# Expert routing moved from its own block into the last batch of the attention, four tiles at a time, with a table by expert and rank

## The chip, the cores and the metric

The kernel runs on one core of a Trainium2 chip. The metric is device time in microseconds (us) of that core, from runs of the whole program. TensorE is called PE here, VectorE DVE, ScalarE ACT, GpSimd POOL and SyncE, which issues most DMAs, SP.

## The reference

One decoder layer over 8 x 256 tokens of width 512: a linear attention, a masked cross attention with 16 heads (both with a residual and a layer norm), and a mixture of 16 experts with the best four per token. What the change touches is the third part:

```python
logits = x @ router_weight.T + router_bias
top_val, top_idx = jax.lax.top_k(logits, TOP_K)
top_val = jax.nn.softmax(top_val, axis=-1)
router_scores = jnp.zeros_like(logits).at[jnp.arange(T)[:, None], top_idx].set(top_val)
gate_up = jnp.einsum('th,ehd->etd', x, gate_up_proj) + gate_up_proj_bias[:, None, :]
...
out = jnp.einsum('etd,edh->eth', (up + 1.0) * glu, down_proj) + down_proj_bias[:, None, :]
out = out * router_scores.T[:, :, None]
out = out.sum(axis=0)
```

## The kernel before, in words

The program is a row of blocks. At the end of a block every engine waits for all the others.

**`attention`** holds the first two parts. The cross attention goes through 8 batches (b) of 16 steps (s), four steps to a group of four heads. In a step PE makes two pairs of score matmuls (`scores`, L1219) into a ring of three PSUM banks (`RING`, `ring_bank`), ACT takes the exponential of each (`exps`, L705), PE multiplies those of two steps earlier with v (`values`, L1236), and PE makes the maxima's scores eight steps ahead (`scores_max`, L1204), which DVE reduces at once (`reduces`, L896), one pair of banks `ps_a` for each half. PE takes no further scores of the maxima until DVE has reduced the last ones. After the last batch's heads are made (`keep_o`), `spread_heads` (L1250) lays them out for two tiles of 128 tokens, DVE inverts the sums (L937), adds (L944 to L949) and normalizes. The tokens of tile t are `x[:, t]`, called x_keep in the profile. The order of all this is written out by hand in the loops over n of each engine; in the last batch `turn_x2` (L1260) turns tiles 10, 11, 12 and 13 at steps 4, 5, 14 and 15, and tiles 14 and 15 at the very end; `logits` (L1270) makes the router's logits of two tiles. POOL finishes the heads of the batch before (`finish_heads`, six instructions, L523 to L531), and raises variances to the power -1/2 (L536, L654, L658).

**`route`** begins when the logits of all 16 tiles stand. SP loads the first expert's weights (12 pieces, L1765), the biases, and stores all of x as the start of the sum (L1590) and zeros for the dummy rows (L1593, L1594), then loads the second expert's weights. ACT and POOL cut the first expert's weights in a high and a low part (`split_hi` L1776, `split_lo` L1785). DVE finds the best four of each token, PE ranks each choice among the earlier ones of its expert (L1724, L1726), DVE turns the ranks into places, an expert's places beginning at a multiple of 128 behind those of the expert before it. For each of 16 tiles DVE then makes two tables of ones and zeros (L1687, L1690) and a product (L1693), ACT another (L1617), and eight matmuls (L1734) add the tokens and their weights up to a list of 79 tiles of 128 places.

**`experts`** goes through those tiles, four to a round. ACT writes the numbers of the rows (`aim_from`, L1940), POOL gathers the rows three tiles ahead (`gather`, L1876), PE turns them (L2051) and makes three products of 12 matmuls (L2070): gate, up and, for the tile before, down. With the first tile of an expert, ACT and POOL also cut the next expert's weights. The weight of each row comes from the tables `weight` and `weight_a`. POOL scatters the results (L1886). **`last_norm`** is the last layer norm.

## Time and profile before

| what | us |
|---|---|
| median of three runs | 1603.31 (1599.92 to 1605.49) |
| the profiled execution | 1600.59 |
| its span | 1598.8 |
| busy PE / DVE / POOL / ACT | 1456.5 / 971.5 / 839.9 / 723.2 |
| matmuls of the experts, three groups of 912 | 231.8, 230.2, 231.6 |
| score maxima reduced by DVE, 256 | 300.3 |

The span is the profiled execution from its first to its last instruction. Times in the trace count from its start. A busy share is a mean over stages with different limits, so the stages are read one by one: the last batch up to 753, the end of the attention up to 769.7, the routing block up to 827.7, and the experts.

### The profile page before, as it was taken

Reading aid. Unit: us, or ns where it says so; the run is one execution under the profiler, and the core shown is the slowest. Engines: PE = TensorE matmul, PEld = TensorE weight load, DVE = VectorE, ACT = ScalarE, POOL = GpSimd, SP = SyncE. Lnnn points to the kernel's source line nnn. Section 1 sums busy time; section 2 is a strip of 40 time slices with the busy share of each in tenths; the row PEclk is TensorE's granted clock in tenths of the full one; section 3 lists DMA queues with packets and bytes.
Section 4 is the critical chain, followed back from the end, with each engine's and each line's share of the span. In section 5 each row is a group of like instructions: output and inputs, shape, how many; then the busy total and the mean of one; then the engine's idle time right before and its main releaser. Section 6 shows DMA issues by size and latency. Waiting matters only on the chain. (4 is left out here: it accounts for less than half of the span.)

```text
span 1598.8 us, 28732 instructions
## 1 busy us (share of the span) xinstructions
PE 1456.5 (91%) x7582; PEld 1031.8 (65%) x7583; DVE 971.5 (61%) x1389; ACT 723.2 (45%) x1348; POOL 839.9 (53%) x681
## 2 busy tenths in 40 slices
PE   6999999799999999998269999999999999999990
PEld 5878887444444444442257887777777877877770
DVE  2324344778887888886765555555555555555554
ACT  4212222278777778775223434424434443444223
POOL 4425333555666765632415536666666666486322
PEclk9999999799999999999579999999999999999996
DMA  6201022564557547530724445655556565473326
GB/s 212 72 14 49 13 49 54 80 89 72 99 113 123 109 84 132 89 64 30 275 75 121 118 92 151 160 151 155 151 151 158 148 161 151 110 191 80 59 54 223
DMA packets 92658, 179.04 MB, mean 112 GB/s; under 512 B 17032, under 2 KB 19848, under 8 KB 91944
## 3 DMA queue, kind: packets, MB, share of 16 engines
q1 hardware_dynamic: 72888, 132.76, 32.8%
q0 software_dynamic: 18544, 44.84, 14.2%
q8 instruction: 38, 0.62, 0.2%
q10 hardware_dynamic: 1152, 0.52, 0.2%
q14 instruction: 36, 0.29, 0.1%
HBM read 115.03 MB, written 33.46 MB: 93 GB/s over the span
## 5 line engine op out<-in xcount | busy, mean ns | idle before, releaser
L896 DVE TENSOR_REDUCE stage<-ps_a 128x2 f32<-128x1024 f32 x256 | 300.3, 1218 | 80.2 <-PE ps_a L1204 79.6
L705 ACT ACTIVATE probs<-ps_b 128x512 f32<-128x512 f32 x512 | 278.0, 595 | 54.4 <-PE ps_b L1219 52.0
L1785 POOL TENSOR_TENSOR we_split<-we_raw,we_split 128x512 f32 (+1 forms) x192 | 250.5, 1543 | 97.3 <-ACT we_split L1776 95.2
L2070 PE MATMUL ps_y<-we_split,hT 128*128 x912 | 231.8, 403 | 4.3 <-DVE hT L2001 3.4
L2070 PE MATMUL ps_g<-we_split,xT 128*128 x912 | 230.2, 401 | 5.0 <-issue 4.3
L2070 PE MATMUL ps_u<-we_split,xT 128*128 x912 | 231.6, 403 | 0.0
L2070 PEld LDWEIGHTS ps_g<-we_split,xT 128*128 128x128 f32 x912 | 171.8, 190 | 52.9 <-issue 12.9
L2070 PEld LDWEIGHTS ps_y<-we_split,hT 128*128 128x128 f32 x912 | 166.2, 189 | 41.8 <-issue 7.2
L2070 PEld LDWEIGHTS ps_u<-we_split,xT 128*128 128x128 f32 x912 | 166.3, 189 | 34.8
L1936 ACT ACTIVATE hT<-ps_h 128x512 fp32r<-128x512 f32 x76 | 45.3, 597 | 296.5 <-PE ps_h L2051 240.3
L1886 POOL DMA_INDIRECT scratch_acc<-x_keep,to_rows x76 | 121.2, 1595 | 109.7 <-issue 51.6
L1219 PE MATMUL ps_b<-stack 55*128 55x512 f32 x512 | 131.0, 505 | 15.9 <-ACT probs L705 11.1
L1236 PE MATMUL ps_pv<-probs,v_aug 128*32 128x512 f32 x1024 | 139.7, 619 | 0.0
L1876 POOL DMA_INDIRECT x_rows<-scratch_x,from_rows x79 | 78.7, 997 | 112.7 <-ACT from_rows L1940 86.1
L1219 PEld LDWEIGHTS ps_b<-stack 55*128 55x128 f32 x512 | 50.8, 188 | 132.1 <-ACT probs L705 114.4
L2022 DVE TENSOR_TENSOR ps_g<-ps_g,we_bias 128x512 f32<-128x512 f32 x76 | 53.2, 700 | 115.7 <-PE ps_g L2070 80.4
L2013 DVE SCALAR_TENSOR_TENSOR x_keep<-ps_y,slot_weight_a,bw 128x512 f32<-128x512 f32 x76 | 57.1, 751 | 95.2 <-PE ps_y L2070 91.9
L2028 DVE TENSOR_TENSOR ps_u<-ps_u,we_bias 128x512 f32<-128x512 f32 x76 | 53.2, 700 | 88.4 <-PE ps_u L2070 88.4
L1930 ACT ACTIVATE xT<-ps_x 128x512 fp32r<-128x512 f32 x78 | 46.8, 600 | 119.0 <-PE ps_x L2051 119.0
L1204 PE MATMUL ps_a<-stack 53*128 53x512 f32 x512 | 90.9, 422 | 10.3 <-DVE stage L896 10.3
L1318 PE MATMUL ps_b<-stack,xT_split 128*128 128x512 f32 x384 | 93.2, 394 | 0.0
L1776 ACT ACTIVATE we_split<-we_raw 128x2048 f32 (+1 forms) x48 | 88.4, 1904 | 3.1 <-DMA we_raw<-in_w_expert 3.1
(254 smaller groups left out, 2213.8 us busy)
## 6 DMA issues: line engine op xcount, KB each, us to landing
we_raw<-in_w_expert SPq DMA_DIRECT2D x192, 256.0 KB
stack<-xT_raw SPq DMA_DIRECT2D x192, 128.0 KB, 5.4
we_bias<-in_b_expert SPq DMA_DIRECT2D x16, 768.0 KB, 4.0
stage<-in_w SPq DMA_DIRECT2D x5, 1024.0 KB, 4.9
xT_raw<-in_xT SPq DMA_DIRECT2D x4, 1024.0 KB, 6.4
x_tok<-in_x POOLq DMA_DIRECT2D x16, 256.0 KB, 3.1
scratch_acc<-x_keep SPq DMA_DIRECT2D x1, 4096.0 KB, 18.0
acc_sb<-scratch_acc SPq DMA_DIRECT2D x8, 512.0 KB, 6.6
```

The lines of the kernel that those rows point to most:

```text
L705: nc.scalar.activation(probs[:, n % 3, h], src[:], ACT.Exp, scale=DH ** -0.5).then_inc(b_kept, 1)
L896: nc.vector.tensor_reduce(out[:, :, i, k % NC], ps_a[i][:], AX.X, ALU.max, negate=True).then_inc(a_kept[i], 1)
L1204: mm = nc.tensor.matmul(ps_a[i][:, e], q_stack[rows, slot, p, c * P:(c + 1) * P], k_stack[rows, slot, p, :], start=True, stop=True)
L1219: nc.tensor.matmul(out[:], k_stack[rows, slot, p, c * P:(c + 1) * P], q_stack[rows, slot, p, :], start=True, stop=True).then_inc(b_made, 1)
L1236: mm = nc.tensor.matmul(ps_pv[32 * h:32 * h + 32, :], v_aug[:, b % 2, c, 4 * g + h, :], probs[:, n % 3, h], start=(c == 0), stop=(c == NC ...
L1318: mm = nc.tensor.matmul(out[:], xT_split[:, xi, c, i * P:(i + 1) * P], w_split[w][:, wi, c, :], start=(n == 0), stop=(n == 3 * KC - 1))
L1776: nc.scalar.activation(dst, W["raw"][:, k], ACT.Copy).then_inc(W["hi"], 1)
L1785: nc.gpsimd.tensor_tensor(lo, W["raw"][:, k, c], hi, ALU.subtract).then_inc(W["lo"], 1)
L1876: pool.indirect_dma_start(x_rows[j][:], None, S["x2"], bass.IndirectOffsetOnAxis(from_rows[j][:], 0))\
L1886: pool.indirect_dma_start(S["acc"], bass.IndirectOffsetOnAxis(to_rows[j][:], 0), y[j], None, compute_op=ALU.add).then_inc(added, 16)
L2013: nc.vector.scalar_tensor_tensor(y[j], ps_y[:], pick(W["weight_a"], i), bw[:, j % 2], ALU.mult, ALU.add).then_inc(y_ready, 1)
L2070: mm = nc.tensor.matmul(out[:], left[:, a, c], w[:, bass.ds(par, 1), k, b, c].squeeze(1), start=(n == 0), stop=(n == len(passes) - 1))
```

## The change

The routing is cut into four groups of four tiles. Groups 0 to 2 are routed inside the last batch of the attention, group 3 in the block `route`.

- DVE: `top_experts`, `chosen_experts` and `rank_slots` of a group take the place of the long instructions over all 16 tiles. Each instruction whose result the next one needs is followed by a wait (`chain`). PE ranks a group with two matmuls (`rank_tokens`); ACT copies the ranks out of the ring and takes the exponentials (`keep_rank`, `raise_shares`).
- A choice's place is now expert x 16 + rank / 128 in a table of 256 columns, so the matmuls that add up the table (`spread_tile`, four to a tile, fp32r) need no totals. Their operands are products of digit tables (`mark_tile`, two instructions to a tile): on POOL for tiles 0 to 11, on DVE for the last four. The table lies in the bank that held the attention's values.
- `route` loses the 16-tile loop. A few small instructions and matmuls turn the counts into `tile_place`, `tile_expert` and the rest. Of the first expert's weights POOL cuts there only the gate's, and only after all marks; up and down are cut at the start of `experts`, behind the first three gathers. The second expert's load moves to the start of `experts`.
- The rows' weights are stored beside x in DRAM (`store_weights`, 32 more columns, so a gathered row has 544 elements). ACT picks a tile's weights from the gathered rows (`keep_weight`) with one register load, and `aim_from` and `aim_to` have a register load each for the place.
- From step 8 of the last batch the ring of scores has five banks: the three, and the two of `ps_a[0]`, free once the last maxima are reduced. `spread_heads` uses `ps_a[1]` alone for both tiles. `make_head_rows` moves ahead of the last reduction.

```diff
+        WIDER = USE["exp", N - LEAD, 0]
+        late_ring = [ps_b[(WIDER + i - EARLY) % RING][:] for i in range(RING)] + [ps_a[0][:, 0], ps_a[0][:, 1]]
...
+                if b == B - 1:
+                    pool.wait_ge(b_made, USE["exp", STEPS * b - 1, 3] + 1)
+                    for t in range(8):
+                        mark_tile(nc.gpsimd, pool, R, K, t, in_tiles[t], of_tiles[t])
                 if b >= 1:
                     finish_heads(b - 1)
...
+            for t in range(8, 10):
+                mark_tile(nc.gpsimd, pool, R, K, t, in_tiles[t], of_tiles[t])
             pool.wait_ge(y2_moments, B - 1)
             nc.gpsimd.tensor_tensor(rstd2[:], mean_var2[:, :, 1], minus_half2[:], ALU.pow).then_inc(y2_rstd, 1)
             for o in range(2):
+                if o == 1:
+                    for t in range(10, EARLY_TILES):
+                        mark_tile(nc.gpsimd, pool, R, K, t, in_tiles[t], of_tiles[t])
...
                 b, s = n // STEPS, n % STEPS
+                if b == B - 1 and s == 7:
+                    make_head_rows()
                 if n + LEAD < N:
                     reduces(n + LEAD)
...
+                    top_experts(nc, dve, R, K, s // 2, s // 2)
+                if b == B - 1 and s in (1, 3):
+                    chosen_experts(nc, dve, R, K, s // 2, s // 2)
+                if b == B - 1 and s in (5, 6):
+                    dve.wait_ge(b_kept, USE["rank", s - 5] + 1)
+                    rank_slots(nc, dve, R, K, s - 5, s - 5, K["rank"][:, (s - 5) % 2])
+            dve.wait_ge(b_kept, USE["logits", 5] + 1)
+            top_experts(nc, dve, R, K, 2, 2)
+            chosen_experts(nc, dve, R, K, 2, 2)
             invert_spread(0)
             invert_spread(1)
             moments(B - 2)
...
             add_spread(0)
+            dve.wait_ge(b_kept, USE["rank", 2] + 1)
+            rank_slots(nc, dve, R, K, 2, 2, K["rank"][:, 0])
             dve.wait_ge(y2_rstd, B - 1)
...
+def mark_tile(compute, engine, R, K, t, in_tile, of_tile, at=None):
...
+    if t % 4 == 0:
+        engine.wait_ge(R["slots_made"], t // 4 + 1)
+    compute.tensor_tensor(in_tile.rearrange("p k (m l) -> p k m l", l=16),
+                          K["mid_tok"][:, at, ks].unsqueeze(3).to_broadcast([P, K_TOP, 8, 16]),
+                          K["low"][:, at, ks].unsqueeze(2).to_broadcast([P, K_TOP, 8, 16]),
+                          ALU.mult).then_inc(R["marked"], 1)
+    compute.tensor_tensor(of_tile, K["chosen"][:, at, ks].unsqueeze(3).to_broadcast([P, K_TOP, E_, n]),
+                          K["hi"][:, at, ks, 0:n].unsqueeze(2).to_broadcast([P, K_TOP, E_, n]),
+                          ALU.mult).then_inc(R["marked"], 1)
...
+            pool.wait_ge(R["marked"], 2 * NT)
+            split_lo(nc, pool, W, 0, 0, 0, range(KC))
```

DVE, the second half of the last batch's steps with maxima. Before, the engine goes from the reductions to the head rows and the inversions (stage<-ps_a are the reduced maxima, kv_mask the head rows, full the inverted sums):

```order
L896 TENSOR_REDUCE stage<-ps_a 128x2 x6
L905 CAST stage<-stage 128x2x8
L907 TENSOR_TENSOR stage<-stage 128x2x8
L930 COPY kv_mask<-ident 128x128
L937 RECIPROCAL full<-ps_a 64x512 x2
L918 BN_STATS stats<-late 128x6 x2
```

Now, from step 6 on:

```order
L934 TENSOR_REDUCE stage<-ps_a 128x2 x2
L1718 TENSOR_TENSOR stage<-stage,w_qk 128x256
L1719 TENSOR_REDUCE stage<-stage 128x16
...
L1734 TENSOR_TENSOR stage<-stage,token 128x128
L968 COPY kv_mask<-ident 128x128
L934 TENSOR_REDUCE stage<-ps_a 128x2 x2
L943 CAST stage<-stage 128x2x8
L945 TENSOR_TENSOR stage<-stage 128x2x8
L1676 TENSOR_TENSOR logits<-logits,rb 128x64
...
L1702 COPY carry<-stage 128x16
L975 RECIPROCAL full<-ps_a 64x512 x2
```

The inversions stand behind all of group 1's slots (L1718 to L1734, eleven instructions) and group 2's choices (L1676 to L1702, 15 instructions).

POOL, the last batch. Before:

```order
L523 TENSOR_TENSOR late<-late,u_sb 128x512 x2
L527 TENSOR_TENSOR late<-late 128x512 x2
L531 TENSOR_TENSOR late<-late,x_keep 128x512 x2
L654 TENSOR_TENSOR rstd<-mean_var,minus_half 128x2
L658 TENSOR_TENSOR rstd<-mean_var,minus_half 128x1 x2
```

Now (L1747 and L1751 are `mark_tile`'s two instructions; of the 16 for tiles 0 to 7 the last two are shown):

```order
L1747 TENSOR_TENSOR in_tile_low<-stage 128x512
L1751 TENSOR_TENSOR stack<-stage,w_qk 128x512
L543 TENSOR_TENSOR late<-late,u_sb 128x512 x2
L547 TENSOR_TENSOR late<-late 128x512 x2
L551 TENSOR_TENSOR late<-late,x_keep 128x512 x2
L1747 TENSOR_TENSOR in_tile_low<-stage 128x512
L1751 TENSOR_TENSOR stack<-stage,w_qk 128x640
L1747 TENSOR_TENSOR in_tile_low<-stage 128x512
L1751 TENSOR_TENSOR stack<-stage,w_qk 128x640
L680 TENSOR_TENSOR rstd<-mean_var,minus_half 128x2
```

The heads of batch 6 stand behind the marks of tiles 0 to 7, and the power for tiles 12 and 13 behind the marks of tiles 8 and 9.

## Rows read from the trace of the kernel before

**Rows 1.** Windows by stage: length, busy time of each engine, TensorE's granted clock, DMA share, GB/s.

```profile
697.00:728.00 31.00, 25.72 (x157) 10.65 (x157) 24.32 (x27) 20.19 (x40) 14.16 (x11) 0.90 0.15 41
769.00:828.00 59.00, 24.85 (x134) 21.25 (x134) 53.79 (x144) 15.23 (x23) 16.90 (x15) 0.70 0.59 215
845.00:1545.00 700.00, 693.67 (x3252) 557.52 (x3251) 403.13 (x593) 270.48 (x490) 416.68 (x327) 1.00 0.53 134
```

**Rows 2.** Timeline of DVE, end of the last batch: start, us, instruction, idle before.

```profile
724.59 1.19 DVE L907 TENSOR_TENSOR stage<-stage 128x16 fp32r<-128x16 f32 x1
725.71 1.35 DVE L930 COPY kv_mask<-ident 128x128 f32<-128x128 f32 x1
729.13 3.35 DVE L937 RECIPROCAL full<-ps_a 64x512 f32<-64x512 f32 x1 [2.08 <-PE ps_a L1250]
737.34 3.36 DVE L937 RECIPROCAL full<-ps_a 64x512 f32<-64x512 f32 x1 [4.86 <-PE ps_a L1250]
742.33 0.17 DVE L923 TENSOR_SCALAR mean_var<-mean_var 128x2 f32<-128x2 f32 x1
744.50 1.00 DVE L962 TENSOR_SCALAR x_keep<-late,mean_var,rstd 128x512 f32<-128x512 f32 x2
```

**Rows 3.** Timeline of POOL: heads of batch 6, power for tiles 12 and 13, first expert's weights.

```profile
725.71 2.48 POOL L531 TENSOR_TENSOR late<-late,x_keep 128x512 f32<-128x512 f32 x2
742.58 1.13 POOL L654 TENSOR_TENSOR rstd<-mean_var,minus_half 128x2 f32<-128x2 f32 x1 [14.39 <-DVE mean_var L923]
777.74 16.45 POOL L1785 TENSOR_TENSOR we_split<-we_raw,we_split 128x512 fp32r<-128x512 f32 x12 [7.60 <-ACT we_split L1776]
```

**Rows 4.** Groups by line and shape, 690 to 820: busy us, mean ns, idle before.

```profile
L1645 DVE TENSOR_REDUCE sel<-chosen 128x256 f32<-128x1024 f32 x1 | 1.9, 1871 | 0.0
L1635 DVE MAX8 top<-logits 128x8 f32<-128x16 f32 x16 | 1.3, 158 | 0.1
L1131 DVE TENSOR_TENSOR logits<-logits,rb 128x256 f32<-128x256 f32 x1 | 0.4, 424 | 4.2 <-ACT logits L724 4.2
L1639 DVE TENSOR_TENSOR gap<-top 128x64 f32<-128x64 f32 x1 | 0.2, 209 | 0.0
```

**Rows 5.** Timeline of DVE in the routing block, beside POOL's twelve instructions of rows 3.

```profile
783.31 0.22 DVE L1656 TENSOR_REDUCE total<-share 128x16 f32<-128x64 f32 x1
788.40 1.17 DVE L1669 TENSOR_TENSOR base<-tile_end,n_tiles 128x16 f32<-128x16 f32 x1
790.82 0.42 DVE L1671 TENSOR_TENSOR place<-ps_r,base 128x256 f32<-128x256 f32 x1
```

**Rows 6.** Timeline of ACT: pairs of exponentials in a step without maxima.

```profile
738.68 1.09 ACT L705 ACTIVATE probs<-ps_b 128x512 f32<-128x512 f32 x2 [1.28 <-PE ps_b L1219]
741.35 1.09 ACT L705 ACTIVATE probs<-ps_b 128x512 f32<-128x512 f32 x2 [0.22 <-PE ps_b L1219]
```

**Rows 7.** Routing block: SP's last store and POOL's first instruction; landing times from the DMA view.

```profile
769.78 0.20 POOL L1602 MEMSET ones<- 128x128 f32 x1 [5.70 <-POOLq L104]
787.41 2.70 SPq L1594 DMA_DIRECT2D scratch_acc<-zero  x1
scratch_acc<-zero SPq DMA_DIRECT2D x1, 256.0 KB, 9.8
```

**Rows 8.** Start of the experts: first instruction, last of three gathers, first product.

```profile
827.73 0.10 POOL L1899 MEMSET zero_row<- 128x1 f32 x1 [33.55 <-POOLq L1527]
831.20 0.95 POOL L1876 DMA_INDIRECT x_rows<-scratch_x,from_rows  x1 [0.30 <-issue]
836.92 5.07 PE L2070 MATMUL ps_g<-we_split,xT 128*128 x12 [1.24 <-issue]
```

**Rows 9.** A tile in which the next expert's weights are cut.

```profile
1039.87 0.19 ACT L1940 ACTIVATE from_rows<-slot_token 128x1 uint32 x1
1039.96 0.58 ACT L1936 ACTIVATE hT<-ps_h 128x512 fp32r<-128x512 f32 x1
1040.57 0.69 DVE L2001 TENSOR_TENSOR hT<-ps_h,hT 128x512 fp32r<-128x512 f32 x1 [0.16 <-ACT hT L1936]
1042.27 3.04 PE L2070 MATMUL ps_y<-we_split,hT 128*128 x12
```

More of the change, by code:

```diff
@@ new lines, in choice_buffers, with sb, chain @@
+def choice_buffers(nc, ctx):
+    def sb(name, shape, dt=F32):
+        return ctx.enter_context(nc.sbuf_tensor(f"late_{name}", shape, dt))[:]
+    views = {name: sb(name, (P, 1) + shape) for name, shape in CHOICE_SHAPES}
+    for name, shape in CHOICE_TEMPS:
+        views[name] = sb(name, (P,) + shape, U32 if name == "top_i" else I32 if name in ("slot_i", "digit_i") else F32)
+    views["hi"] = sb("hi", (P, 1, 4 * K_TOP, E_))
+    views["ones"] = sb("ones", (P, P))
+    return views
+def chain(R, dve, instruction):
+    R["done"][0] += 1
+    instruction.then_inc(R["step"], 1)
+    dve.wait_ge(R["step"], R["done"][0])
@@ new lines, in spread_tile, with raise_shares @@
+def spread_tile(nc, pe, R, table, t, in_tile, of_tile):
+    pe.wait_ge(R["marked"], 2 * t + 2)
+    columns = table[:, 0:PLACES].rearrange("p (e h) -> p e h", e=E_)[:, :, 0:of_tile.shape[-1]]
+    for k in range(K_TOP):
+        mm = nc.tensor.matmul(columns, in_tile[:, k], of_tile[:, k], start=(t == 0 and k == 0),
+                              stop=(t == NT - 1 and k == K_TOP - 1), skip_group_check=True)
+    mm.then_inc(R["spread_done"], 1)
+def raise_shares(nc, act, R, gap, g):
+    act.wait_ge(R["sel_made"], g + 1)
+    nc.scalar.activation(gap, gap, ACT.Exp).then_inc(R["raised"], 1)
@@ new lines, in store_weights, with tile_tables, sb @@
+def store_weights(sp, S, R, weights, g, groups):
+    sp.wait_ge(R["weights_made"], 1 if g == 0 else 2)
+    rows = S["x2"][4 * g * P:4 * (g + groups) * P, D:D + 2 * E_]
+    sp.dma_start(rows.rearrange("(t p) e -> p t e", p=P), weights.rearrange("p g t x -> p (g t) x")).then_inc(
+        R["weights_stored"], 16)
+def tile_tables(nc, ctx):
+    def sb(name, shape, dt):
+        return ctx.enter_context(nc.sbuf_tensor(name, shape, dt))
+    return {
+        "token": sb("place_token", [P, PLACES + 1], U32),
+        "place": sb("tile_place", [1, TILES], I32),
+        "expert": sb("tile_expert", [1, TILES], I32),
+        "active": sb("tile_active", [1, TILES], I32),
+        "new": sb("tile_new", [1, TILES], I32),
+        "parity": sb("tile_parity", [1, TILES], I32),
+        "last_tile": sb("expert_last", [1, E_], I32),
+    }
@@ L1963, in _ @@
                 aim_from(j, j)
-            x_hi(0, 0)
-            x_hi(1, 1)
+            for j in range(2):
+                x_hi(j, j)
+                keep_weight(j, j)
             def body(i, j):
@@ L1981, in body @@
                 weigh_bias(i, j, par)
+                if not (isinstance(i, int) and i >= TILES - 2):
+                    keep_weight(i + 2, (j + 2) % U)
                 if not is_at(i, 0):
```

491 lines of the change are left out of this document (282 added, 209 removed).

## The prediction

> **What bounds the kernel now.** I read the windows by stage first. In the experts PE is busy 693.67 of 700 us [rows 1]: there only PE's work counts, and the change leaves it alone. In the routing block PE has 24.85 of 59 us and DVE 53.79: DVE's row of instructions is that block, 58.0 us from POOL's first instruction at 769.78 to the first of the experts at 827.73 [rows 7, 8]. The last batch comes next. There PE has 25.72 of 31 us, DVE 24.32 and POOL 14.16 [rows 1]. PE cannot make the maxima's scores of a step before DVE has reduced those of the last one, so DVE has only 31 - 24.3 = 6.7 us to give before it holds PE. Then I read the timelines of DVE and POOL there, because that is where the work goes, and asked which chain leads to the end: head rows, two inversions, moments, power on POOL, and x_keep of tiles 12 and 13 at 744.50 [rows 2], which PE needs in step 14 and without which nothing behind it (turn, logits, spread, tiles 14 and 15) starts.
>
> **The end of the attention, up to the first inversion.** DVE gets, before its inversions, three times `top_experts`, three times `chosen_experts` and twice `rank_slots`. From the groups [rows 4]: an instruction of 64 columns takes 0.21, of 256 columns 0.42, the sixteen MAX8 1.3 together, the strided reduction of 1024 columns 1.87, and I give each `chain` wait 0.04.
> - `top_experts`: 0.21 + four MAX8 0.4 + four index searches 0.6 (an estimate, half as much again as the MAX8) + 0.21 + 0.2 + gaps = 1.7, three times 5.1.
> - `chosen_experts`: 0.42 + a quarter of 1.87 = 0.5 + a scan of 80 columns and two small copies 0.5 + gaps = 1.6, three times 4.8.
> - `rank_slots`: three of 256 columns 1.3, a reduction 0.4, two of 128 columns 0.6, five small ones 0.7, gaps 0.3 = 3.3, twice 6.6.
> - constants 0.9. Sum 17.4 us if nothing else runs.
>
> Something else runs. While POOL does its twelve instructions of 1.2 to 1.4 us (16.45 in all), an instruction of 16 columns takes DVE 1.17 us, where a reduction takes 0.22 and one with a PSUM operand 0.42 [rows 3, 5]. The same shows at 724.59 and 725.71, beside POOL's heads: 1.19 and 1.35 [rows 2, 3]. So a small DVE instruction that reads SBUF twice, or copies, waits for the end of POOL's current one, about 1.0 us each. The change puts 16 marks and the six heads, some 24 us of POOL work without a break, beside DVE from the moment group 0's slots are made: beside group 1's slots (7 instructions of the waiting kind until POOL runs out of marks for group 0), two of the maxima, and the 8 such of group 2's choices. That is 17 with those; three of them more or less, and three waits are there today (two of some 1.1 in these rows, and the cast ahead of them: 2.9 together), so 17 x 1.0 - 2.9 = 14.1.
>
> The Trainium skill says the same as a rule against this change (SBUF — State Buffer, Who interferes with whom): VectorE with two SBUF inputs, or in a 2-port mode, and GpSimd reading SBUF lock each other out for a whole instruction. The rows above bear it out, reductions and PSUM operands included. Read alone, it would let me price a wait at half an instruction, 0.6 us; then the 17 cost 10 in place of 17 and the whole comes out near 1600. The rows show nearly the full length each time, since DVE's next instruction arrives just after POOL's next has begun, so I keep 1.0.
>
> The first inversion, now at 729.13, so moves by 17.4 + 14.1 - 6.7 (DVE's idle time) - 2.1 (its wait for the spread heads, [rows 2]) + 1 for handovers that stay = 23.7 us.
>
> **Up to tiles 12 and 13.** The second inversion waits 4.86 us for step 10 today [rows 2]; by then it will not: -4.9. The heads of batch 6 end at 728.2 today [rows 3]; behind the marks they end some 30 later, at about 758, still ahead of the moments. From the variance (742.50) to x_keep (744.50) it is 2.0 us now, since the power (1.13) runs beside `add_spread`. Then it will be `add_spread` 2.1 with its handovers, `rank_slots` of group 2 3.3, POOL's marks of tiles 8 and 9, 2 x (1.25 + 1.55 for 640 columns) = 5.6, the power 1.1, handovers 0.3: 12.4, so +10.4. Sum: 23.7 - 4.9 + 10.4 = 29.2.
>
> **The ring of five.** Two pairs of exponentials take 2 x 1.09 = 2.2 us, and a step 741.35 - 738.68 = 2.7 [rows 6]: the ring could give 0.5 x 8 = 4 us. I count nothing, as PE will stand in step 14 for x_keep anyway, some 20 us. The head rows' move ends a stall of PE at step 8, with the same answer. `spread_heads` on one pair waits for `add_spread(0)`, done before x_keep: nothing.
>
> **Behind x_keep.** 24 us lead from 744.50 to the last logits today. They stay, and PE starts them after a long wait; in the routing block, where it waits as much, it was granted 0.70 of its clock [rows 1]. Add twelve table matmuls (tiles 9 to 11) before the last logits: +0.7, `share_weights` partly hidden, colder matmuls +1. Sum +1.7. The attention ends 29.2 + 1.7 = 31 us later.
>
> **The routing block.** DVE's row is then: choices of group 3 with constants 3.8, weights 1.7, slots 3.3, marks 4 x (0.7 + 1.2) = 7.6 (512 and 1024 columns, estimates by 0.42 for 256), counts and tables about 9, of which 4 are waits beside POOL's four cuts: 26 us with the start. But SP's zeros, issued at 787.41, land 9.8 later, at 797.2, which is 27.5 us after the block's start [rows 7], behind the same 3 MB of weights and 4 MB of x that stay. So the DMAs become the block's end: 27.5 + 0.8 for the last weights and the barrier = 28.3, in place of 58.0: -29.7. Bounds: 27.5 if the small store lands in time, 34 if DVE's small instructions wait more often.
>
> **The experts.** The first product starts 9.2 us after the block does [rows 8]. It now needs POOL's low part of the up weights, cut behind the third gather: 831.20 + 0.95 + 4 x 1.25 + 0.3, that is 9.7 to 10: +1 with what follows on ACT in the first tile. `keep_weight` and two register loads stand ahead of the cut of the next expert's weights. In such a tile ACT's hT starts at 1039.96, DVE's part ends at 1041.26, and PE comes to it at 1042.27 [rows 9]: 0.9 us of slack with the handover in each of 14 changes of expert. No row shows a load alone; from below nothing, as three loads between two ACT instructions at 1039.87 and 1039.96 cost nothing seen; from above some 2 us a tile, 14 x 1.2 = 17. I take +1, nearest to the row. The 6% longer gathered row costs nothing at a DMA share of 0.53.
>
> **Sum.** 31 - 29.7 + 1 + 1 = +3.3 us, so 1603.9 for the profiled execution of 1600.59. The median of the runs is 2.7 above that execution, so I forecast 1606.6, rounded to **1607**: the routing block loses half its time and the last batch gets it all back. About 0.3% (4.8 us) can be told from no change, so the line lies at 1598.5 and 1608.1.
>
> **Rivals.**
> - *The work hides (faster).* If DVE's small instructions seldom meet POOL's, the 14.1 goes; DVE then waits for batch 6's heads behind the marks, which gives back about 4. The attention ends 21 later, time 1597; if the slots' own 10 us hid too, 1588. For it: DVE has 6.7 us idle, and 7 more in its waits for spread heads. Against: two rows of 1.19 and 1.35 in this very place.
> - *The marks cost more than 1.25 us (slower).* They have four-dimensional broadcast operands, and no row shows one on POOL. Tiles 0 to 7 hold DVE and the heads, tiles 8 and 9 lie in the chain itself. At 1.3 times the price the chain grows by 6.5 us (3 in waits on DVE and the heads, 1.7 in tiles 8 and 9, the rest in tiles 10 and 11 ahead of the last power), time 1613; at 1.6 times by 15, 1622. Slower than can be missed from 1.1 times on.
> - *Register loads in the experts (slower).* 14 x up to 1.2 us: up to 1624. For it nothing but the order of instructions.
>
> **Chances.** Forecast, 1599 to 1615: 0.50, of which 0.28 within 0.3% and 0.22 above. Hidden: 0.30, all faster. Marks: 0.15. Loads: 0.05. Faster 0.30, same 0.28, slower 0.42. The range 1590 to 1622 leaves out the deepest part of the first rival and the ends of the other two; the forecast's own is 1599 to 1615.
>
> **What would show it.** The routing block 28 us long, its end released by a DMA. DVE's first inversion 20 us or more later against step 0 of the last batch, small instructions of 1.0 to 1.3 us beside POOL's marks. PE idle for more than 10 us before the turn of tile 12, released by x_keep. Pairs of exponentials closer together than 1.35 us in steps 9 to 13. Wrong would be: x_keep of tile 12 less than 20 us later, marks far from 1.25 us for 512 columns, or an experts' stage longer by over 3 us.

## The result, and the profile of the changed kernel

| | kernel before | changed kernel |
|---|---|---|
| median of 20 runs each, us | 1600.7 | 1605.5 |
| all runs, us | 1592.9 to 1607.0 | 1603.5 to 1609.4 |
| profiled span, us | 1598.8 | 1604.6 |
| ratio of the times | | 1.0035, 95% interval 1.0023 to 1.0047 |

The change makes the kernel slower by 0.35%, just more than the 0.3% that can be told from no change. The forecast was 1607, and 0.42 stood on slower. But the sum that gave it was right only as a whole: the last batch up to the first inversion was forecast 7.7 us too high and the experts 8.6 us too low. That the two cancel is luck.

This is where the time went, from one profile of each kernel. The marks in time are ACT's first exponentials of the last batch (693.89 and 692.45), DVE's first inversion, the variance and x_keep of tiles 12 and 13, POOL's first instruction of the routing block, POOL's first of the experts, the 76 instructions of DVE that finish a tile (`finish`), and the end.

| stretch | before | after | difference | forecast |
|---|---|---|---|---|
| up to step 0 of the last batch | 693.9 | 692.5 | -1.4 | 0 |
| from there to DVE's first inversion | 35.2 | 51.3 | +16.0 | +23.7 |
| from there to the variance | 13.2 | 8.4 | -4.8 | -4.9 |
| variance to x_keep of tiles 12, 13 | 2.2 | 10.8 | +8.6 | +10.4 |
| x_keep to the routing block | 25.3 | 28.9 | +3.6 | +1.7 |
| routing block | 58.0 | 28.5 | -29.5 | -29.7 |
| experts, to the first finished tile | 28.8 | 32.2 | +3.3 | +1 |
| first to 75th tile, 15 changes of expert | 700.0 | 707.3 | +7.3 | +1 |
| the last interval | 6.8 | 9.6 | +2.8 | 0 |
| behind the last tile | 35.5 | 35.4 | -0.1 | 0 |
| sum | | | +5.8 | +3.3 |

The two marks of step 0, the kernel before first:

```profile
693.89 1.09 ACT L705 ACTIVATE probs<-ps_b 128x512 f32<-128x512 f32 x2 [0.89 <-PE ps_b L1219]
```

```profile
692.45 1.09 ACT L734 ACTIVATE probs<-ps_b 128x512 f32<-128x512 f32 x2 [0.39 <-PE ps_b L1279]
```

Windows by stage of the changed kernel, with the columns of [rows 1]: the last batch up to the first inversion, the routing block, the experts.

```profile
697.00:744.00 47.00, 37.20 (x201) 13.98 (x193) 45.17 (x114) 26.08 (x55) 25.34 (x25) 0.89 0.10 28
791.00:820.00 29.00, 7.16 (x34) 5.37 (x34) 18.53 (x66) 6.18 (x5) 5.15 (x5) 0.50 0.91 331
845.00:1545.00 700.00, 688.44 (x3209) 550.00 (x3208) 397.14 (x584) 286.46 (x556) 414.37 (x326) 1.00 0.54 135
```

In the last batch DVE is now busy 45.17 of 47 us: it became the bound, and its idle time of [rows 1] is used up. In the experts the same 700 us hold 5.2 us less of PE's work than before. The share of busy time falls from 99.1% to 98.3%, too little to notice on the page, but as large as the whole loss.

The timeline of DVE in the last batch, against [rows 2]:

```profile
725.81 0.42 DVE L1719 TENSOR_REDUCE stage<-stage 128x16 f32<-128x256 f32 x1
726.26 0.83 DVE L1720 CAST stage<-stage 128x16 int32<-128x16 f32 x1
...
735.54 0.41 DVE L1678 MAX8 stage<-logits 128x8 f32<-128x16 f32 x4
...
738.56 1.47 DVE L1690 TENSOR_TENSOR stage<-iota_f,stage 128x256 f32<-128x256 f32 x1
...
743.70 6.74 DVE L975 RECIPROCAL full<-ps_a 64x512 f32<-64x512 f32 x2
...
752.08 0.17 DVE L961 TENSOR_SCALAR mean_var<-mean_var 128x2 f32<-128x2 f32 x1
...
762.83 1.00 DVE L1000 TENSOR_SCALAR x_keep<-late,mean_var,rstd 128x512 f32<-128x512 f32 x2 [5.42 <-POOL rstd L680]
```

and of POOL, against [rows 3]: the two marks of tile 7 (L1747 and L1751), the heads of batch 6, then marks of tiles 8 and 9 and the power.

```profile
736.41 1.05 POOL L1747 TENSOR_TENSOR in_tile_low<-stage 128x512 fp32r<-128x512 f32 x1
737.42 1.06 POOL L1751 TENSOR_TENSOR stack<-stage,w_qk 128x512 fp32r<-128x512 f32 x1
738.45 2.70 POOL L543 TENSOR_TENSOR late<-late,u_sb 128x512 f32<-128x512 f32 x2
...
758.51 1.29 POOL L1751 TENSOR_TENSOR stack<-stage,w_qk 128x640 fp32r<-128x640 f32 x1
...
762.01 0.72 POOL L680 TENSOR_TENSOR rstd<-mean_var,minus_half 128x2 f32<-128x2 f32 x1
```

The cast of 16 columns takes 0.83 us beside a mark, where the free one takes 0.17. The four MAX8 and the reduction keep their 0.41 and 0.42: they are not held. The two inversions stand back to back, so PE's spread heads are no longer waited for. And x_keep waits 5.42 us for POOL, which makes marks from 757.50 on and comes to the power at 762.01.

PE behind it (the views' line numbers are those of the changed kernel; L1761 is `spread_tile`):

```profile
763.43 1.11 PE L1321 MATMUL ps_b<-ident,x_keep 128*128 128x128 f32 x4 [12.45 <-DVE x_keep L1000]
...
779.78 6.24 PE L1761 MATMUL table<-stack,in_tile_low 128*128 128x64 f32 x28
785.82 1.05 PE L1321 MATMUL ps_a<-ident,x_keep 128*128 128x128 f32 x4
```

PE stands 12.45 us, then works almost without a break to the end of the stage. x_keep of tile 15 is there at 781.9, but its turn comes at 785.82, behind the products of tiles 2 to 8.

The routing block ends as forecast. These are the last issue of SP, DVE's last instruction and POOL's first of the experts, and from the DMA view the landing time of the last store:

```profile
812.41 2.67 SPq L1793 DMA_DIRECT2D scratch_x<-late_weights  x1
812.48 0.23 DVE L1916 SCALAR_TENSOR_TENSOR tile_new<-expert_f,new_f 1x79 int32<-1x79 f32 x1
820.15 0.10 POOL L2100 MEMSET zero_row<- 128x1 f32 x1 [8.02 <-POOLq L1817]
```

```profile
scratch_x<-late_weights SPq DMA_DIRECT2D x1, 64.0 KB, 7.3
```

DVE is through at 812.7; the last store, issued at 812.41, lands 7.3 us later, and the block ends at 820.15.

In the experts the difference sits at the changes of expert. ScalarE before and after in the same tile (the kernel before first), from the bias over the cuts of the next expert's weights to the next hT:

```profile
1204.47 0.71 ACT L1950 ACTIVATE bw<-we_bias,slot_weight 128x512 f32 x1
1205.09 0.19 ACT L1944 ACTIVATE to_rows<-slot_token 128x1 uint32 x1
1205.18 5.51 ACT L1776 ACTIVATE we_split<-we_raw 128x2048 f32 x3
1210.59 0.19 ACT L1940 ACTIVATE from_rows<-slot_token 128x1 uint32 x1
1210.68 0.58 ACT L1936 ACTIVATE hT<-ps_h 128x512 fp32r<-128x512 f32 x1
```

```profile
1205.18 0.71 ACT L2165 ACTIVATE bw<-we_bias,row_weight 128x512 f32 x1
1205.79 0.19 ACT L2158 ACTIVATE row_weight<-x_rows 128x2 f32 x1
1206.21 0.20 ACT L2152 ACTIVATE to_rows<-place_token 128x1 uint32 x1 [0.23 <-issue]
1206.59 5.53 ACT L1975 ACTIVATE we_split<-we_raw 128x2048 f32 x3 [0.17 <-issue]
1212.01 0.18 ACT L2147 ACTIVATE from_rows<-place_token 128x1 uint32 x1
1212.10 0.58 ACT L2139 ACTIVATE hT<-ps_h 128x512 fp32r<-128x512 f32 x1
```

The cuts start 0.71 us behind the bias before, 1.41 after. The loads in front of `from_rows` cost nothing here, hidden behind 5.5 us of cuts. hT is 0.7 later against the bias, and then PE:

```profile
1217.31 3.06 PE L2288 MATMUL ps_g<-we_split,xT 128*128 x12 [0.58 <-issue]
```

Before, the same gate product follows the down product at once; now it comes 0.58 us late. In an undisturbed tile the interval is 9.27 us in both kernels; in this one it is 10.13 against 9.41.

### The profile page after: what moved, and what is told of

Same layout as the page of the kernel before. It is cut to its first block and busy times, and to the rows that moved or that the text cites. A ratio compares the mean times of both kernels' runs of the same rounds, so it can differ in the third digit from the quotient of the medians.

```text
span 1604.6 us, 29621 instructions
## 1 busy us (share of the span) xinstructions
PE 1454.8 (91%) x7542; PEld 1028.6 (64%) x7543; DVE 966.7 (60%) x1414; ACT 738.4 (46%) x1416; POOL 862.1 (54%) x704
## 5 line engine op out<-in xcount | busy, mean ns | idle before, releaser
L734 ACT ACTIVATE probs<-ps_b 128x512 f32<-128x512 f32 x498 | 270.5, 595 | 50.3 <-PE ps_b L1279 44.1
L2288 PE MATMUL ps_y<-we_split,hT 128*128 x912 | 235.4, 407 | 6.0 <-DVE hT L2219 3.5
L1279 PE MATMUL ps_b<-stack 55*128 55x512 f32 x498 | 127.7, 502 | 16.7 <-ACT probs L734 8.2
L1296 PE MATMUL table<-probs,v_aug 128*32 128x512 f32 x1024 | 138.8, 615 | 0.5 <-ACT o_pair L742 0.5
L2231 DVE SCALAR_TENSOR_TENSOR x_keep<-ps_y,row_weight,bw 128x512 f32<-128x512 f32 x76 | 57.1, 751 | 94.1 <-PE ps_y L2288 94.1
L1264 PE MATMUL ps_a<-stack 53*128 53x512 f32 x512 | 90.2, 417 | 15.7 <-DVE stage L934 15.4
```

The lines of the kernel that those rows point to most:

```text
L734: nc.scalar.activation(probs[:, n % 3, h], src[:], ACT.Exp, scale=DH ** -0.5).then_inc(b_kept, 1)
L1264: mm = nc.tensor.matmul(ps_a[i][:, e], q_stack[rows, slot, p, c * P:(c + 1) * P], k_stack[rows, slot, p, :], start=True, stop=True)
L1279: nc.tensor.matmul(out[:], k_stack[rows, slot, p, c * P:(c + 1) * P], q_stack[rows, slot, p, :], start=True, stop=True).then_inc(b_made, 1)
L1296: mm = nc.tensor.matmul(ps_pv[32 * h:32 * h + 32, :], v_aug[:, b % 2, c, 4 * g + h, :], probs[:, n % 3, h], start=(c == 0), stop=(c == NC ...
L2231: nc.vector.scalar_tensor_tensor(y[j], ps_y[:], weight[:, j, 1:2], bw[:, j % 2], ALU.mult, ALU.add).then_inc(y_ready, 1)
L2288: mm = nc.tensor.matmul(out[:], left[:, a, c], w[:, bass.ds(par, 1), k, b, c].squeeze(1), start=(n == 0), stop=(n == len(passes) - 1))
```

## The experiments

Each line of a diff is against the changed kernel, if nothing else is said. First four that undo or move one part, in one series; the kernel before took 1599.9 there.

**1. The power ahead of the marks.**

```
-            for t in range(8, 10):
-                mark_tile(nc.gpsimd, pool, R, K, t, in_tiles[t], of_tiles[t])
             pool.wait_ge(y2_moments, B - 1)
...
-                    for t in range(10, EARLY_TILES):
+                    for t in range(8, EARLY_TILES):
...
             add_spread(0)
-            dve.wait_ge(b_kept, USE["rank", 2] + 1)
-            rank_slots(nc, dve, R, K, 2, 2, K["rank"][:, 0])
...
             last_norm(B - 1, 0, last_step)
+            dve.wait_ge(b_kept, USE["rank", 2] + 1)
+            rank_slots(nc, dve, R, K, 2, 2, K["rank"][:, 0])
```

> The changed kernel, with the power for tiles 12 and 13 issued on POOL ahead of the marks of tiles 8 and 9 (these go behind the power of tile 14), and the third rank_slots on DVE behind the normalization of tile 14. Nothing is left out. Theory: x_keep of tiles 12 and 13 is late because DVE ranks group 2 (754.2 to 757.4 in the changed kernel) and POOL makes two pairs of marks (757.5 to 762.0) before the power. With the swap x_keep follows the residual add at once: 754.3 plus about 0.8 for the power, so at about 755 instead of 762.8, and since PE stands 12.45 us there and works almost without a break behind it, the attention ends 7 to 8 us earlier: 1598 us. Rival A: the time behind x_keep is set by DVE (inversions of 3.4 us, the rank now between them, and waits beside POOL), which gives 3 to 4 us of it back: 1602. Rival B: x_keep 7 us earlier moves nothing, since PE's own work up to the end was what counted: 1605.

Measured: 1598.4 us, ratio to the kernel before 0.9994 (0.9983 to 1.0005), where the changed kernel has 1.0035: 6.6 us less (8.5 against the second series' 1.0047 of run 5). x_keep stands at 757.91 here; PE's turn in it:

```profile
758.50 0.88 PE L1319 MATMUL ps_b<-ident,x_keep 128*128 128x128 f32 x4 [3.30 <-DVE x_keep L998]
```

From the first inversion (747.36 here) to x_keep it takes 10.6 us in place of 19.1, so 8.6 less: the term of the table. From x_keep to the block it takes 28.5, as before the edit. The theory holds, and both rivals fall.

**2. ScalarE's order in the experts.**

```
...
                 nc.scalar.activation(glu[:], ps_g[:], ACT.Silu, scale=ALPHA).then_inc(glu_made, 1)
+                if not (isinstance(i, int) and i >= TILES - 1):
+                    keep_weight(i + 1, (j + 1) % U)
+                if not below(i, 2):
+                    aim_to(i - 2, (j - 2) % U)
                 if not (isinstance(i, int) and i >= TILES - 2):
                     x_hi(i + 2, j)
                 weigh_bias(i, j, par)
-                if not (isinstance(i, int) and i >= TILES - 2):
-                    keep_weight(i + 2, (j + 2) % U)
-                if not is_at(i, 0):
-                    aim_to(i - 1, (j - 1) % U)
...
```

> The changed kernel, with the experts' ScalarE order changed alone: the copy of a row's weights and the aiming of the scatter, with the register loads ahead of them, stand behind the SiLU, where ScalarE waits 1.5 us for PE, instead of between the bias and the cut of the next expert's weights. Nothing is left out. Theory: of the changed kernel's 5.8 us over the kernel before, 7.4 us arise at the 15 changes of expert, 0.5 us each: the cuts start 0.70 us later, the next hT is late by as much, PE's down product is released later and its sequencer has no lead left at the loop's branch (a gap of 0.58 us in front of the gate product). With the cuts where they were these gaps shrink to those of the kernel before: 6 to 7 us less, 1599 us. Rival A: the register loads cost wherever they stand (ScalarE or the loop's branch carries them): 1605. Rival B: the gaps come from the 544-wide gathers or the earlier weight loads, not from ScalarE: 1605 too, with hT on time.

Measured: 1600.0 us, ratio 1.0001 (0.9988 to 1.0014). The 74 intervals take 701.7 us, against 707.3 in the changed kernel and 700.0 before. ScalarE in a tile with a change, behind the cuts:

```profile
1207.82 0.59 ACT L2139 ACTIVATE hT<-ps_h 128x512 fp32r<-128x512 f32 x1
1208.39 0.60 ACT L2194 ACTIVATE glu<-ps_g 128x512 f32<-128x512 f32 x1
1209.10 0.21 ACT L2158 ACTIVATE row_weight<-x_rows 128x2 f32 x1
1209.80 0.20 ACT L2152 ACTIVATE to_rows<-place_token 128x1 uint32 x1 [0.49 <-issue]
```

The loads are still there, and cost 0.49 us and more of ScalarE's time, but in its wait for PE. 5.6 of the 7.3 us are gone. Both rivals fall: the loads and the copy cost by their place, and gathers and weights' loads are as in the changed kernel. The run does not part the loads from the copy `keep_weight`, which moves with them.

**3. A ring of three banks.**

```
-        late_ring = [ps_b[(WIDER + i - EARLY) % RING][:] for i in range(RING)] + [ps_a[0][:, 0], ps_a[0][:, 1]]
+        late_ring = [ps_b[(WIDER + i - EARLY) % RING][:] for i in range(RING)]
```

> The changed kernel with three banks in the ring of scores for the last steps too, as in the kernel before. Nothing is left out. Theory: the ring of five lets PE reach the turn of tile 12 earlier (751.0 in the changed kernel), where it stands 12.45 us for DVE, so the two banks are worth nothing: 1605.5, within 0.3% of the changed kernel, with a shorter stand before the same turn. Rival: the wider ring feeds DVE's last row maxima and the heads earlier, so that without it the heads' inversion is later by a step's difference: 1608 to 1612.

Measured: 1606.6 us, ratio 1.0036 (1.0024 to 1.0049): the same as the changed kernel. PE's stand in front of the turn of tile 12 shrinks from 12.45 us to 8.67:

```profile
768.21 1.12 PE L1321 MATMUL ps_b<-ident,x_keep 128*128 128x128 f32 x4 [8.67 <-DVE x_keep L1000]
```

What the steps lose is taken from the wait. From step 0 of the last batch to the first inversion it takes 53.7 us here. Five profiles with the ring of five and the same code up to there have 51.3 to 53.3, so the rival has nothing for it that this run could tell from the spread.

**4. The accumulator stored early.**

```
             store_x2(B - 3)
+            sp.dma_start(S["acc"][0:(NT - 4) * P, :].rearrange("(t p) d -> p t d", p=P),
+                         x[:, 0:NT - 4, :]).then_inc(x2_stored, 16)
...
-            sp.dma_start(S["acc"][0:TOK, :].rearrange("(t p) d -> p t d", p=P), x[:]).then_inc(acc_stored, 16)
+            sp.dma_start(S["acc"][(NT - 4) * P:TOK, :].rearrange("(t p) d -> p t d", p=P),
+                         x[:, NT - 4:NT, :]).then_inc(acc_stored, 16)
```

> The changed kernel, with the accumulator's rows of tiles 0 to 11 (3 MB of 4 MB) stored during the last steps of the attention, where the DMA engines are busy for 0 to 20% of the time, instead of in the routing block. Nothing is left out. Theory: the routing block of 28.5 us waits for its transfers (DVE is through at 812.7, the block ends at 820.15, the DMA engines are full from about 800 on); with 3 MB at 406 GB/s less, 7.4 us of transfers go, and the block ends where DVE and the last store of weights (landed about 815) set it: 5 us less, 1600.5 us. Rival A: the end is set by the descriptors of the zeros, 9.89 us of issue, not by the bytes: 1604 to 1605. Rival B: the early store delays the stores of x_keep and the last loads of the attention, and gives the gain back: 1605.

Measured: 1600.3 us, ratio 1.0001 (0.9988 to 1.0013), so 5.4 us less. The block runs from 792.48 to 814.00, 21.5 us in place of 28.5. SP and DVE in it:

```profile
800.68 0.62 SPq L1860 DMA_DIRECT2D scratch_x<-zero  x1
```

```profile
813.28 0.23 DVE L1919 SCALAR_TENSOR_TENSOR tile_new<-expert_f,new_f 1x79 int32<-1x79 f32 x1
```

DVE's last instruction ends 0.5 us ahead of the barrier: the bound passed from the transfers to DVE. Note the issue of the zeros: 9.89 us in the changed kernel, 0.62 here with the same descriptors. It shrank with the bytes ahead of it, so rival A took a wait for work. The block gains 7.0 us and the whole 5.4; 0.7 of the difference is that the first product comes 12.0 us after the experts' start in place of 11.3: PE takes up the first gathered rows 5.7 us after the gather is issued, in place of 5.0.

**5. The changed kernel again**, in a second series with runs 6 to 8; the kernel before took 1600.4 there.

> The changed kernel again, unchanged, beside the next three on one chip. Theory: what differs from run to run of one kernel is the early attention (up to 2.4 us between two profiles of edits that do not touch it) and whether PE's clock has fallen before the very last product (9.59 us against 6.8 us of the last interval between two results). So this run gives 1605.5 within 1.5 us, intervals of 9.59 or less at the end, and 707 to 708 us for the 74 intervals before it. Rival: those 707 us are themselves luck of a profile, and another one shows 700 to 703 as the kernel before.

Measured: 1608.7 us, ratio 1.0047 (1.0030 to 1.0064), 3.2 us above the 1605.5 that I gave and outside the 1.5 us that I allowed. The 74 intervals take 707.7 us, the last 8.5. The first inversion comes at 747.47, 3.8 us later than in the first profile. 3.5 of that lie ahead of the last batch: from its step 0 on it is 51.5 us here and 51.3 there. So times of single profiles are compared here from mark to mark only.

**6. The kernel before with the register loads.** The diff is against the kernel before; `own` holds each tile's own number.

```
             def aim_to(i, j):
-                nc.scalar.activation(to_rows[j][:], pick(G["token"], i), ACT.Copy).then_inc(to_set, 1)
+                at = act.value_load(pick(W["own"], i), min_val=0, max_val=TILES - 1)
+                nc.scalar.activation(to_rows[j][:], pick(G["token"], at), ACT.Copy).then_inc(to_set, 1)
...
+            def keep_like(i, j):
+                e = act.value_load(pick(G["expert"], i), min_val=0, max_val=E_ - 1)
+                nc.scalar.activation(kept[:, j], pick(G["weight"], e), ACT.Copy)
...
                 weigh_bias(i, j, par)
+                if not (isinstance(i, int) and i >= TILES - 2):
+                    keep_like(i + 2, (j + 2) % U)
```

(`aim_from` likewise.)

> The kernel before, with the register loads of the change alone: on ScalarE the aiming of gather and scatter goes through a table that holds each tile's own number (one more register load each, which the copy's address depends on), and a copy of 128x1 at an address from a loaded register stands between the bias and the aiming of the scatter. Nothing is left out and the results are the same. Theory: ScalarE in front of the cuts is what the experts' 7.4 us come from, so the kernel before takes on 6 to 7 us: 1606 to 1607 us, with the cuts 0.7 us behind the bias and gaps in front of the gate product of 0.58 us. Rival: the loads cost only together with the gathers of 544 columns or the earlier weights: below 1602.

Measured: 1610.0 us, ratio 1.0066 (1.0047 to 1.0085), so 9.6 us more than the kernel before, where I had expected 6 to 7. The 74 intervals take 707.6 us against 700.0, and look like those of the changed kernel. Another 1.8 stand ahead of the first finished tile: the first gather is issued 0.6 us later behind the register loads, and the first down product takes 4.59 us in place of 3.06. ScalarE at a change:

```profile
1207.33 0.71 ACT L1957 ACTIVATE bw<-we_bias,slot_weight 128x512 f32 x1
1207.95 0.19 ACT L1951 ACTIVATE row_kept<-slot_weight 128x1 f32 x1
1208.38 0.20 ACT L1947 ACTIVATE to_rows<-slot_token 128x1 uint32 x1 [0.24 <-issue]
1208.76 5.52 ACT L1778 ACTIVATE we_split<-we_raw 128x2048 f32 x3 [0.18 <-issue]
```

It is 1.43 us from bias to cuts, as good as the 1.41 of the changed kernel, without a wider gather and with the old order of the weights' loads. With run 2 this settles it: the cause is what stands on ScalarE ahead of the cuts, a copy and register loads together. Which of the two costs more was not tested.

**7. The table's bank free.** On top of run 1:

```
+                if s == 14 and b == B - 1:
+                    pe.wait_ge(o_kept, NG * B - 1)
+                    for t in range(0, 8):
+                        spread_tile(nc, pe, R, table, t, in_tiles[t], of_tiles[t])
                 if s in (4, 5, 14, 15) and b == B - 1:
                     turn_x2(2 * b - 4 + (4, 5, 14, 15).index(s))
```

and the last head group's sums in `ps_a[0][:, 1]`, which leaves the ring.

> The kernel of the run with the power first, with the last head group's values summed in one of the two banks that the ring of five had taken (the ring has four), so that the place table's bank is free, and the products that spread tiles 0 to 7 stand ahead of the turn of tile 12, where PE waits, instead of behind the turn of tile 14. Nothing is left out. Theory: behind x_keep of tile 12 PE works without a break up to the end, and 6.5 us of that are these products; PE has 3.3 us of waiting in front of the turn, so 3.3 us are gained and the rest is only moved: 1595 us. Rival A: the products delay the turn of tile 12, the spreading of heads 2 and DVE's last inversions by 3 us, and DVE's chain from there (invert, add, moments, power) is what ends the attention: no gain, 1598.4. Rival B: four banks in place of five let the steps before lag by over 2 us: 1600.

Measured: 1598.0 us, ratio 0.9984 (0.9972 to 0.9996), where run 1 has 0.9994: 1.6 us less, not 3.4, and the two intervals overlap, so the times alone do not show a gain. From x_keep of tile 12 to the block it takes 26.3 us in place of 28.5, so 2.2 less. The last turn now waits for DVE and no longer behind products:

```profile
775.89 1.12 PE L1323 MATMUL ps_b<-ident,x_keep 128*128 128x128 f32 x4 [0.40 <-DVE x_keep L999]
```

So the theory and rival A were each partly right: PE's own work was the bound, and after 2.2 us DVE's chain of the last tiles took over.

**8. All four edits together.**

> The changed kernel with all four edits together: the power first, ScalarE's order in the experts, the accumulator's rows of tiles 0 to 11 stored early, the table's bank free and the products of tiles 0 to 7 ahead of the turn of tile 12. Nothing is left out. Theory: they touch different stretches (attention's end, experts, routing block) and add up: 7 + 5.7 + 5.3 + 3 us off 1605.5, so 1584.5 us, faster than the kernel before by 1%. Rival: the routing block that starts earlier waits for the weights' load or DVE in any case, and the experts' first product is bound by the weights of the first expert, so that only 12 to 14 us come through: 1592.

Measured: 1582.0 us, ratio 0.9875 (0.9854 to 0.9896). The attention's gain, the block of 21.5 us and 700.3 us for the 74 intervals are all there. By stretches of the profiles the parts add up, each in its own: 8.6 + 2.2 + 7.0 + 7.0 = 24.8 us, where the ratios give 25.6. By whole times they do not quite: the single runs gave 8.2 (run 7 with run 1 in it), 5.4 and 5.4, so 19.0. The four executions of this run leave 22 to 29, and the rest is not explained. This version beats both kernels: by 18 us the kernel before, beside which it ran, and by 1.6% the changed one, by their ratios.

**9. No marks beside the ranking.** On top of run 1:

```
                     pool.wait_ge(b_made, USE["exp", STEPS * b - 1, 3] + 1)
-                    for t in range(8):
-                        mark_tile(nc.gpsimd, pool, R, K, t, in_tiles[t], of_tiles[t])
...
-                    for t in range(8, EARLY_TILES):
+                    for t in range(EARLY_TILES):
```

> The kernel of the run with the power first, with the marks of tiles 0 to 7 also moved, behind POOL's power of tile 14, so that POOL works on nothing but the heads while DVE ranks group 1 and chooses the experts of group 2. Nothing is left out. It is not meant to be faster: POOL then makes all 24 marks behind the power, about 24 us, and PE's products wait for them. Theory: DVE's small instructions of 0.8 to 1.5 us (rank_slots of group 1 took 5.6 us against 3.25 us for the same of group 0, the choice of group 2 9.3 us against 3.5 us) are waits beside POOL's marks and heads; without the marks the ranking takes 3.3 us again, and the first inversion comes 18 to 21 us behind the inversion of batch 6 instead of 27; the choice stays slow where it lies beside POOL's heads. The whole takes 1603 to 1612. Rival: the instructions are slow for another reason (the clock, the ring, their own data), keep their durations, and the first inversion stays at 27.

Measured: 1603.4 us (one run), the first inversion 23.5 us behind the inversion of batch 6 (718.48 to 741.97), not 26.9 as in the changed kernel or 27.5 as in run 1, but outside my 18 to 21. The details are the opposite of what I wrote. Without the marks POOL's heads, released earlier, lie beside the ranking of group 1, and the choice of group 2 is free:

```profile
726.65 2.89 POOL L543 TENSOR_TENSOR late<-late,u_sb 128x512 f32<-128x512 f32 x2 [15.61 <-PE ps_b L1275]
```

```profile
732.07 1.20 DVE L1720 CAST stage<-stage 128x48 f32<-128x48 int32 x1
733.30 1.29 DVE L1727 TENSOR_TENSOR stage<-iota_f,stage 128x128 f32<-128x128 f32 x1
734.63 0.43 DVE L1728 TENSOR_TENSOR w_qk<-iota_f,stage 128x256 f32<-128x256 f32 x1
...
739.80 0.21 DVE L1678 TENSOR_TENSOR stage<-logits,stage 128x64 f32<-128x64 f32 x1
```

The ranking takes 8.7 us in place of 5.6, the choice 3.4 in place of 9.3. So the rival falls: the same instructions are slow or quick with nothing changed but what POOL does at that time. Which of POOL's work it is doesn't matter, but its length does: beside heads of some 1.25 us a held instruction loses 0.5 to 1.1 us here; beside marks of 0.4 to 1.06 us it loses 0.2 to 0.9 in the changed kernel.

## Why the prediction came out, and where its steps did not

The number and the direction came out. The mechanism did so in part: the routing block, the chain to x_keep and the ring were read rightly, and two errors of some 8 us cancelled by luck. Of the prediction's own signs of being wrong, one came plainly: the experts' stage is longer by 10.6 us up to the 75th tile, where 3 was the line. One came narrowly: x_keep of tile 12 is 18.3 us later, or 19.8 from step 0 of the last batch, where less than 20 was to be wrong. The marks of 512 columns take 1.05 us in place of 1.25. The first inversion, which was to be 20 us or more later from step 0, is 16.0 later.

**The first inversion: +23.7 forecast, +16.0 measured** from step 0 of the last batch. The step that failed is "17 x 1.0 - 2.9 = 14.1". In the changed kernel 13 instructions are held by 0.2 us or more, and lose 9.0 us together over their free durations, 0.69 each; minus the 2.9 of before that is +6.1. With it the sum gives 15.7. This is from one pair of profiles: the second profile of the changed kernel has 51.5 us for the stretch, that of run 6, which has the attention of before, 34.1. I had read one row of 1.17 and two of [rows 2] and priced every wait at a whole instruction of POOL. The estimate of 0.6 us, half an instruction, that I had drawn from the Trainium skill (SBUF — State Buffer, Who interferes with whom) and set aside is near the 0.69; as to which instructions are held and which are spared, trace and rule agree. I counted the MAX8, the index searches and the reductions right, as free.

**The second inversion: -4.9.** As forecast, back to back.

**Variance to x_keep: +10.4 forecast, +8.6 measured.** The mechanism is right, and run 1 shows it by taking it away. The term that was mis-sized is the marks: 1.05 us for 512 columns and 1.29 for 640, in place of 1.25 and 1.55. With its broadcast operands a mark is cheaper than the plain subtraction of the weights, not dearer, and with that the rival on the marks' price falls.

**The ring of five: 0.** Right (run 3).

**Behind x_keep: +1.7 forecast, +3.6 measured.** I counted the twelve products of tiles 9 to 11 at 0.7 us. They take 2.7 from the first one's start to the logits, where PE had waited 0.8 before, and put the logits off by 1.4. Those of tiles 2 to 8 hold the last turn for 3.9 us after its x_keep is there; the sum leaves them out without a reason. Against it 1.1 us come back up to that x_keep, and 0.6 behind the logits. The colder matmuls are there (a granted clock of 0.55 from 764.5 to 767.9, near the lower of its two levels, and 3.44 us for the spread heads in place of 1.93), but since DVE's chain still got shorter, the +1 for them was not a cost. Run 7 gets 2.2 us back.

**The routing block: -29.7 forecast, -29.5 measured.** Right in size and in cause: the transfers end it. Run 4 takes bytes away and the block falls to DVE's 21, where I had estimated 26; my DVE row was 5 us too long, which the DMAs hid.

**The experts: +2 forecast, +10.6 measured** to the 75th tile. The step "I take +1, nearest to the row" failed: the changes of expert cost 7.3. The row [rows 9] showed 0.9 us of slack between hT and PE at one change, and 0.70 us of delay would have fitted. At some changes it does not: in tiles where hT was later already, the down product now waits (0.36 and 0.51 us in two such tiles). And there is a second place. Intervals of 10.1 us and more, against 9.27, stand in these two profiles only where the next gate product is the first of a loop's iteration of four tiles (tiles 8, 16, 20 and so on), as in the row with 0.58 us above: five in the kernel before, twelve now. My reading is that PE's sequencer runs ahead of its matmuls and so hides the branch, and that a down product that is released late takes this lead away. That is argued from the rows and was not tested by itself. In runs 1, 2 and 8 four intervals of 10.1 us and more stand elsewhere in the iteration, each where a down product waits about 0.6 us, so such an interval has more than one form. That what stands on ScalarE ahead of the cuts is the cause, runs 2 and 6 show. The size, 0.5 us for each of 15 changes, lies inside the bounds of 0 and 17 that stood there; the middle would have been nearer. The first finished tile is late by 3.3: 2.1 lie before the first product and 1.2 in the first down product, 4.28 us where it took 3.06. The rows, the turn of the kernel before first:

```profile
832.00 1.09 PE L2051 MATMUL ps_x<-ident,x_rows 128*128 128x128 f32 x4 [10.10 <-DMA x_rows<-scratch_x,from_rows]
```

```profile
826.50 1.09 PE L2269 MATMUL ps_x<-ident,x_rows 128*128 128x128 f32 x4 [16.03 <-DMA x_rows<-scratch_x,from_rows]
...
831.43 5.04 PE L2288 MATMUL ps_g<-we_split,xT 128*128 x12 [1.24 <-POOL we_split L1984]
...
848.01 4.28 PE L2288 MATMUL ps_y<-we_split,hT 128*128 x12 [1.84 <-DVE hT L2219]
```

The 2.1 are not POOL's cuts, as the prediction had it and as the releaser in the row at 831.43 suggests: the cuts that this product needs end within 0.02 us of 9.96 us after the block's start in every profile of the new order, and the product starts at 10.9 to 12.0, always 4.9 us behind PE's first turn of gathered rows, as in the kernel before. The turn is what is late, 6.35 us after the start in place of 4.27. Of that 0.6 is the first gather's issue, behind the register loads, and 1.5 its rows, which PE takes up 5.0 us after the issue in place of 3.5. Run 6, with the loads alone, has the 0.6 and 3.5. Whether the 1.5 come from the second expert's weights, which load beside the gather now, or from the wider rows, no run parts. The 1.2 are no cost of the change: the granted clock is 0.67 on the mean there (848.0 to 852.3), so part of it is at the lower of the two levels, and in run 5, the same code, the product takes 3.06.

**The last interval: 0 forecast, +2.8 in the profile.** PE's last product takes 5.48 us, and the windows show a granted clock of 0.53 there, the lower of its two levels (1.2 GHz):

```profile
1563.69 5.48 PE L2288 MATMUL ps_y<-we_split,hT 128*128 x12 [1.66 <-DVE hT L2219]
```

```profile
1565.00:1570.00 5.00, 4.17 (x10) 2.68 (x9) 0.75 (x1) 0.00 (x0) 0.00 (x0) 0.53 0.03 5
```

In the kernel before the same product takes 3.07 at full clock, after PE had stood 1.62 and 1.65 us ahead of its last two pieces of work; here it stood 1.93 and 1.66. The change does not touch this product. Over the profiles of all runs the last interval is 6.5 to 6.8 us in five and 8.3 to 9.6 in six. Three of the five short ones have the changed experts (runs 3, 4 and 9), so I do not count it as a cost of the change. But the two profiles with the order of before are both short, so a part in it is not ruled out.

**The rivals.** "The work hides" was half right: the waits beside POOL took 9.0 us in place of 17, and the attention ended 23.3 us later from step 0 of the last batch (21.9 by the clock of the profile), where that rival said 21 and the forecast 31. Had I taken it and kept the experts at +2, I would have forecast 1597 and been wrong by 8. "Register loads in the experts", to which I gave 0.05, is by itself enough to decide the sign, taken as loads and copy ahead of the cuts: with these elsewhere the kernel is at 1600.0 (run 2), no different from before. Runs 1 and 4 do as much, each with another part.

## What to carry to other kernels

Before a step is spread over an engine that looks idle by its share, count what stands behind it on each queue: here two pairs of marks and a ranking ahead of one power of 0.7 us cost 8.6 us, and one more small copy with register loads ahead of the weights' cuts 7.3. The same loads and copy behind the SiLU, where ScalarE waits for PE anyway, left 1.7 of these, so look first at where they stand. And look at every stage's loss in us rather than at its busy share: here 0.8% of the longest stage outweighed what the sign of the result hung on.

## What the runs showed of the hardware that was not expected

- Beside POOL's marks and heads a small DVE instruction with two inputs in SBUF, or a cast, a copy or a TENSOR_SCALAR there, loses 0.2 to 1.1 us, by the rows according to how long POOL's current one still runs; MAX8, FIND_INDEX8 and the reduction keep their durations beside the same marks (0.41, 0.17 and 0.42 us).
- A ScalarE copy whose address comes from a register that is loaded just ahead of it shows 0.23 to 0.49 us of "issue" in front in the rows above; behind 5.5 us of other work the same load shows nothing.
- The issue of a DMA with many descriptors took 9.89 us with the store of 4 MB ahead of it in the queue and 0.62 us with 1 MB.
- The same code's first inversion differs by 3.8 us between two profiles (743.70 and 747.47), nearly all of it ahead of the last batch, while the 74 intervals of the experts agree within 0.4 us (707.3 and 707.7). With other runs that leave the experts alone they go up to 708.5.
